# Second attention: row sums by a product with ones and one division for eight heads, in place of normalised exponentials

## What is computed

```python
qkv = hidden_states @ qkv_w + qkv_b          # [4, 256, 3 * 512]
q, k, v = split into 32 heads of D = 16
q, k = rope(q), rope(k)
scores = einsum('bqhd,bkhd->bhqk', q, k) / sqrt(16)
scores = scores + (1 - causal) * -66504.0
probs = softmax(scores, axis=-1)
ctx = einsum('bhqk,bkhd->bqhd', probs, v).reshape(b, s, 512)
return ctx @ out_w + out_b
```

## Time and profile before

| | |
|---|---|
| runs | 1877.82 us, the median of 3 (1872.31 to 1882.22) |
| profiled execution | 1872.54 us |
| its span, first to last instruction | 1870.7 us |
| busy in the span | TensorE 1760.0, VectorE 1115.4, ScalarE 1087.4, GpSimd 912.1 us |
| the second attention's steps | about 1555 to 1789 us |
| instructions | 32100 |

### The profile page before, as it was taken

One profiled execution on the slowest core, in us unless ns is written; L12 is line 12 of the kernel. 1 busy time (PEld: TensorE's weight loads), 2 busy tenths in 40 slices (PEclk: granted clock), 3 DMA queues, 4 the chain that ended last, 5 costly groups with the idle time before them and its releaser, 6 DMA issues.

```text
span 1870.7 us, 32100 instructions
## 1 busy us (share of the span) xinstructions
PE 1760.0 (94%) x11076; PEld 1527.0 (82%) x11076; DVE 1115.4 (60%) x3334; ACT 1087.4 (58%) x3071; POOL 912.1 (49%) x1153
## 2 busy tenths in 40 slices
PE   7979999999999999999999999999989788898788
PEld 6769989989998998998999899899878566666566
DVE  5655565556456556555644655654566777777656
ACT  3346565566556656556655765655632446777843
POOL 4545544555444555455554555545522336668720
PEclk9999999999999999999999999999989998999999
DMA  4300021012002001101200210110110310000001
GB/s 136 108 16 18 6 69 35 1 46 63 1 18 74 18 6 62 41 1 40 65 6 18 61 31 1 58 51 1 35 57 23 96 46 1 2 1 24 18 7 45
DMA packets 35424, 65.78 MB, mean 35 GB/s; under 512 B 4032, under 2 KB 4672, under 8 KB 35264
## 3 DMA queue, kind: packets, MB, share of 16 engines
q1 hardware_dynamic: 35264, 63.73, 10.8%
HBM read 61.62 MB, written 2.10 MB: 34 GB/s over the span
## 4 chain that ended last, share of the span: by engine, by line
PE 71%; DVE 9%; ACT 8%; issue 7%; POOL 5%; DMA 0%; SPq 0%; POOLq 0%; DVEq 0%; ACTq 0%
PE bank L357 55%; PE bank L974 5%; PE bank L961 4%; PE bank L976 3%; ACT s L1079 2%; POOL s L1795 2%; PE bank L1510 1%; PE bank L1481 1%; PE bank L1497 1%; DVE h L676 1%; ACT s L1566 1%; ACT W L256 1%; POOL WF L269 1%; POOL W L269 1%; POOL rstd L322 1%
## 5 line engine op out<-in xcount | busy, mean ns | idle before, releaser
L357 PE MATMUL bank<-W,oT 128*128 128x512 f32 x1632 | 432.7, 401 | 1.0 <-DVE oT L1747 1.0
L1286 POOL TENSOR_TENSOR qk<-work,qk 128x512 fp32r<-128x512 f32 (+1 forms) x160 | 193.5, 1209 | 445.9 <-ACT qk L1070 445.9
L357 PEld LDWEIGHTS bank<-W,oT 128*128 128x128 f32 x1632 | 290.1, 190 | 49.3 <-issue 1.3
L1086 ACT COPY pt<-bank 128x384 f32<-128x384 f32 x256 | 122.1, 477 | 329.8 <-PE bank L961 329.5
L1079 ACT ACTIVATE s<-s,neg_max 128x128 f32<-128x128 f32 (+1 forms) x512 | 227.6, 445 | 54.3 <-DVE neg_max L1193 52.1
L1278 POOL TENSOR_TENSOR work<-work,table 128x512 f32<-128x512 f32 (+1 forms) x160 | 191.3, 1196 | 139.1 <-ACT work L1065 139.1
L357 PE MATMUL bank<-W,xnA 128*128 128x320 f32 (+1 forms) x1056 | 186.3, 333 | 3.2 <-DVE xnA L342 2.9
L1170 DVE TENSOR_TENSOR work<-bank,table 128x512 f32<-128x512 f32 (+1 forms) x160 | 102.0, 637 | 132.3 <-ACT work L1065 132.3
L357 PEld LDWEIGHTS bank<-W,xnA 128*128 128x128 f32 x1056 | 166.8, 188 | 16.6 <-DVE xnA L342 4.1
L357 PE MATMUL bank<-xnA,W 128*128 128x256 f32 (+1 forms) x1080 | 162.1, 300 | 8.2 <-DVE W L262 6.8
L357 PE MATMUL bank<-xnB,W 128*128 128x256 f32 (+1 forms) x1080 | 164.3, 302 | 3.3 <-DVE xnB L342 3.3
(11 more groups left out here) (106 smaller groups left out, 3507.3 us busy)
## 6 DMA issues: line engine op xcount, KB each, us to landing
raw<-in_weights SPq DMA_DIRECT2D x215, 256.0 KB, 2.7
x<-in_x SPq DMA_DIRECT2D x8, 256.0 KB, 4.8
out<-x SPq DMA_DIRECT2D x8, 256.0 KB, 2.0
row<-in_bias_rows SPq DMA_DIRECT2D x5, 256.0 KB, 2.7
table<-in_constants SPq DMA_DIRECT2D x4, 240.0 KB, 3.2
b_qk<-in_bias_rows SPq DMA_DIRECT2D x1, 512.0 KB, 3.6
b_val<-in_bias_rows SPq DMA_DIRECT2D x1, 256.0 KB, 3.0
table<-in_constants SPq DMA_DIRECT2D x1, 66.0 KB, 2.3
```

Of the source, the lines that this page charges most:

```text
L357: last = nc.tensor.matmul(out_ap, lhs(i), rhs(j), start=start and k == 0, stop=stop and k == 2)
L1086: nc.scalar.copy(pt0[:, k, :], bank[PT][:, 0:3 * P]).then_inc(a_pt, 1)
L1286: nc.gpsimd.tensor_tensor(lo, work[:, 2 + s, st.columns(what)], hi.bitcast(F32), ALU.subtract).then_inc(a_rope_lo, 1)
```

## The change

The exponentials are no longer normalised before they are turned. TensorE turns them as soon as they are there (`b_exp`), and weighs the values with them as they are. Behind each step's weighting stand eight more products: the turned exponentials once more, with a stationary matrix of ones (32 columns; in the even step ones in its first half and zeros in the other, in the odd step the other way round), into columns 256 to 511 of OUT1. So each of the 128 rows of the group's output has its own row sum beside it, in the same bank. When the group is done, VectorE takes the reciprocal of the 128x256 sums, multiplies the output by it into a buffer `o1` in SBUF, and hands the bank on (`b_divided`). ScalarE makes the high part from `o1`, and GpSimd the low part. The accumulator outputs of the exponentials, the small reciprocals and the normalisation are gone. `divided(n)` is true for all steps, since DIVIDED is 0. GpSimd sets the ones once, by four memsets ahead of step 0.

```diff
--- before.py
+++ after.py
@@ -192,6 +192,8 @@
             b_row_sum = sb(a, "b_row_sum", [P, 8, 2])
             b_inv_sum = sb(a, "b_inv_sum", [P, 8, 4])
             b_val = sb(a, "b_val", [P, DIM])
+            ones = sb(a, "ones", [P, 2, 2 * D1])
+            o1 = sb(a, "o1", [P, 2, SEQ])
 
         bank = [ctx.enter_context(nc.psum_tensor(f"bank{i}", [P, CH], F32)) for i in range(8)]
         ident = table[:, T_ID:T_ID + P]
@@ -1342,6 +1344,9 @@
         b_o_lo = sem("b_o_lo")
         b_out = sem("b_out")
         b_row = sem("b_row")
+        b_ones = sem("b_ones")
+        b_inverse = sem("b_inverse")
+        b_divided = sem("b_divided")
         b_added = sem("b_added")
         LN1 = 32
         LAST_AT = [20, 20, 21, 22, 23, 24, 25, 26, 27, 28, 29]
@@ -1351,6 +1356,7 @@
         QUADS = BATCH * PER_BATCH
         STEPS1 = QUADS + 1
         SLOTS = 8
+        DIVIDED = 0
         ORING = 6
 
         PROJ = [(0, 0), (1, 0), (0, 1), (1, 1), (2, 0), (2, 1)]
@@ -1390,6 +1396,19 @@
             FILL_USES += [fill_of(n)] if fill_of(n) else []
             FILL_USES += [("norm", *norm_of(n))] if norm_of(n) else []
         FILL_USES += [("out", BATCH - 1, 0)]
+
+        def divided(n):
+
+            return n >= DIVIDED
+
+        def sum_read(eng, group):
+
+            if group < 0:
+                return
+            if divided(2 * group):
+                eng.wait_ge(b_divided, group - DIVIDED // 2 + 1)
+            else:
+                eng.wait_ge(b_o_lo, group + 1)
 
         def norm_no(b, tt):
             return LN1 + 2 + 2 * b + tt
@@ -1445,7 +1464,7 @@
 
             group = GR1 * b + g
             pe.wait_ge(b_rope, rope_no(b, 3) + 1)
-            at_least(pe, b_o_lo, group - 1)
+            sum_read(pe, group - 2)
             for j in range(2):
                 for tt in range(2):
                     c = j * DIM + g * P
@@ -1488,7 +1507,7 @@
                 group, odd = divmod(m, 2)
                 if not odd:
                     pe.wait_ge(b_v, group + 1)
-                    at_least(pe, b_o_lo, group)
+                    sum_read(pe, group - 1)
                     pe.wait_ge(b_q, min(group + 2, QUADS // 2))
                 for s in b_pt:
                     pe.wait_ge(s, 2 * (m + 1))
@@ -1497,14 +1516,22 @@
                         last = nc.tensor.matmul(bank[OUT1][rows(j), tt * P:SEQ],
                                                 vz[:, group % 2, odd, tt, 32 * j:32 * (j + 1)],
                                                 pt1[:, j, tt * 2 * P:(tt + 2) * P],
-                                                start=odd == 0 and tt == 0, stop=odd == 1 and tt == 1)
+                                                start=odd == 0 and tt == 0,
+                                                stop=odd == 1 and tt == 1 and not divided(m))
+                if divided(m):
+                    pe.wait_ge(b_ones, 4)
+                    for tt in range(2):
+                        for j in range(4):
+                            last = nc.tensor.matmul(bank[OUT1][rows(j), SEQ + tt * P:2 * SEQ], ones[:, odd, :],
+                                                    pt1[:, j, tt * 2 * P:(tt + 2) * P],
+                                                    start=False, stop=odd == 1 and tt == 1)
                 if odd:
                     last.then_inc(b_pv, 1)
 
             def turn(m, j):
                 if m == 0 and j < 2:
                     pe.wait_ge(b_biased, 5 + j)
-                pe.wait_ge(b_norm, 4 * m + j + 1)
+                pe.wait_ge(b_exp if divided(m) else b_norm, 4 * m + j + 1)
                 at_least(pe, b_pt[j % 2], 2 * m + j // 2)
                 for blk in range(3):
                     last = nc.tensor.transpose(bank[PTB[j % 2]][:, blk * P:(blk + 1) * P],
@@ -1563,9 +1590,12 @@
                 s = (4 * n + j) % SLOTS
                 act.wait_ge(b_min, 4 * n + j + 1)
                 for qt, cols in ((0, slice(0, P)), (1, slice(P, 3 * P))):
-                    last = nc.scalar.activation(s1[:, s, cols], s1[:, s, cols], ACT.Exp,
-                                                bias=b_neg_max[:, s, qt:qt + 1], scale=-1.0,
-                                                accum_out=b_row_sum[:, s, qt:qt + 1])
+                    bias = b_neg_max[:, s, qt:qt + 1]
+                    if divided(n):
+                        last = nc.scalar.activation(s1[:, s, cols], s1[:, s, cols], ACT.Exp, bias=bias, scale=-1.0)
+                    else:
+                        last = nc.scalar.activation(s1[:, s, cols], s1[:, s, cols], ACT.Exp, bias=bias, scale=-1.0,
+                                                    accum_out=b_row_sum[:, s, qt:qt + 1])
                 last.then_inc(b_exp, 1)
 
             here, before = n < QUADS, n >= 1
@@ -1583,8 +1613,12 @@
                 exponentials(3)
             if before and n % 2 == 0:
                 group = n // 2 - 1
-                act.wait_ge(b_pv, group + 1)
-                nc.scalar.copy(oT1[HI][:, group % ORING, :], bank[OUT1][:, 0:SEQ]).then_inc(b_o_hi, 1)
+                if divided(n - 1):
+                    act.wait_ge(b_divided, group - DIVIDED // 2 + 1)
+                    nc.scalar.copy(oT1[HI][:, group % ORING, :], o1[:, group % 2, :]).then_inc(b_o_hi, 1)
+                else:
+                    act.wait_ge(b_pv, group + 1)
+                    nc.scalar.copy(oT1[HI][:, group % ORING, :], bank[OUT1][:, 0:SEQ]).then_inc(b_o_hi, 1)
             if here:
                 b_pt_copy(act, n, 0)
                 b_pt_copy(act, n, 1)
@@ -1731,7 +1765,7 @@
                 b_vector_keys(dve, *prep_of(n - 1))
             if before:
                 b_pt_copy(dve, n - 1, 3)
-            if here:
+            if here and not divided(n):
                 inverses(0)
             if roped:
                 b_vector_cosine(dve, *roped)
@@ -1739,9 +1773,17 @@
                 b_vector_apply(dve, *norms_after(n - 1))
             if fill and fill[0] == "proj":
                 b_vector_biased(dve, *fill[1:])
-            if here:
+            if here and not divided(n):
                 inverses(1)
-            if before and n % 2 == 0:
+            if before and n % 2 == 0 and divided(n - 1):
+                group = n // 2 - 1
+                dve.wait_ge(b_pv, group + 1)
+                at_least(dve, b_o_lo, group - 1)
+                nc.vector.reciprocal(o1[:, group % 2, :], bank[OUT1][:, SEQ:2 * SEQ]).then_inc(b_inverse, 1)
+                dve.wait_ge(b_inverse, group - DIVIDED // 2 + 1)
+                nc.vector.tensor_tensor(o1[:, group % 2, :], bank[OUT1][:, 0:SEQ], o1[:, group % 2, :],
+                                        ALU.mult).then_inc(b_divided, 1)
+            elif before and n % 2 == 0:
                 group = n // 2 - 1
                 dve.wait_ge(b_o_hi, group + 1)
                 nc.vector.tensor_tensor(oT1[LO][:, group % ORING, :], bank[OUT1][:, 0:SEQ],
@@ -1765,6 +1807,10 @@
                 ln_power(pool, norm_no(0, i), i)
             pool.wait_ge(row_loaded, 16 * 4)
             pool.wait_ge(b_zero, 2)
+            for odd in range(2):
+                for half in range(2):
+                    nc.gpsimd.memset(ones[:, odd, half * D1:(half + 1) * D1],
+                                     1.0 if half == odd else 0.0).then_inc(b_ones, 1)
             for n in range(STEPS1):
                 b_gpsimd_step(pool, n)
 
@@ -1812,15 +1858,21 @@
                 b_sine(pool, *roped[1:])
             if n < QUADS and s in VALUES_AT:
                 values(VALUES_AT[s])
-            if n < QUADS:
+            if n < QUADS and not divided(n):
                 normalise(0)
                 normalise(1)
             if n < QUADS and s in (2, 4):
                 tt = s // 2 - 1
                 nc.gpsimd.tensor_tensor(tile_of(b, tt), tile_of(b, tt), row[:, :], ALU.add).then_inc(b_row, 1)
-            if n < QUADS:
+            if n < QUADS and not divided(n):
                 normalise(2)
                 normalise(3)
+            if n >= 1 and n % 2 == 0 and divided(n - 1):
+                group = n // 2 - 1
+                pool.wait_ge(b_o_hi, group + 1)
+                nc.gpsimd.tensor_tensor(oT1[LO][:, group % ORING, :], o1[:, group % 2, :],
+                                        oT1[HI][:, group % ORING, :].bitcast(F32),
+                                        ALU.subtract).then_inc(b_o_lo, 1)
             for i in norms_after(n)[1] if norms_after(n) else ():
                 ln_power(pool, norm_no(norms_after(n)[0], i), i % 2)
             for i in last_splits(n):
```

## The result

The changed kernel takes 1913.4 us, the median of four runs (1909.1 to 1913.9), against 1878.8 for the kernel before: a ratio of 1.0187 (95% interval 1.0163 to 1.0210), so 31 to 39 us slower. A second series gave 1.0207 (1.0185 to 1.0230). The forecast was 33 us slower, 1907 us, with a range of 1886 to 1924. The profiled execution took 1912.97 us.

A forecast was written before the change was run, and what follows sets the result against it. TensorE was taken as the bound. Terms 25.3 + 1.5 + 1.2 + 3.75 + 3.0 + 1.05 + 2.2 - 3.0 - 2.0 gave +33 us: 1905.5 on the profiled execution, 1910.8 on the median; predicted 1907, range 1886 to 1924.

The forecast's parts named there:

- Ones, 25.3 forecast: Eight more TensorE products ahead of the scores in each of 32 steps: +25.3 us, lower end 23.0.
- the row of the same form, 0.79: The weighting's 0.79 us from its start to the scores, taken as the cost of each step's products with ones.
- The reciprocal, 1.55 forecast: VectorE's reciprocal of 256 columns after every second step, from medians of short reciprocals: 1.55 us, bounds 0.80 to 2.4.
- estimate of 2.1 us: The large reciprocal at eight cycles of 0.96 GHz an element: 2.1 us, the sum 9 us higher.
- Even steps: Division alone in steps 2, 10, 12, 18, 20 and 28, followed by a projection: 0.25 us each, +1.5.
- steps 4, 24 and 26: No projection follows; copies, norm or minima are on the path of the division: 1.0 us each, +3.0.
- 14 and 22 by 1.9 and 6: Steps with moments behind the division on VectorE, then minima, exponentials, masks, weighting: 1.25 us each, +3.75.
- 8 and 16: Steps with norm, then projection; the norm's cast is late behind ScalarE's copies: 0.6 us each, +1.2.
- The gain, 5 forecast: Time won back: 3.0 us from GpSimd's normalisation, 2.0 from accumulator reads at 0.4 in steps 5, 6, 14, 22, 30.
- the transposing matmuls waited 7.2 us in all: TensorE's transposes waited 7.2 us for GpSimd's normalisation; about 3 us credited, in steps 21, 28 and 31.
- 10.5 for the steps: The division's delays in the even steps: 1.5, 1.2, 3.75 and 3.0 us, and 1.05 in step 30.
- The end, 3.0 forecast with its ones: Behind the last weighting: division, cast and GpSimd's subtraction take 3.3 us where 1.1 stood, +2.2 without the ones.
- rival 3: New waits of ScalarE in light steps drop TensorE's clock in eight more such steps: +12, 1918 us; chance 0.10.

The follow-up runs named there:

- the first run: The kernel before, still normalised, with the products with ones added behind each weighting and their result unused: ratio 1.0091, median 1890.8 us.

## Why the prediction was right

The direction and the mechanism were right: both new costs were put where they are, and TensorE's plain odd steps pay for the ones in full. The size was right in part by luck: the ones were put 4.5 us too dear and the division, less what it relieves, 6.5 too cheap, which mostly cancelled, and 3 us at the end were missing. The medians are 34.6 us apart. The two profiled executions are 40.4 us apart: 32.1 in the 31 steps, 6.1 behind them, and 3.0 ahead of the first weighting, which starts anywhere from 1565.7 to 1573.9 us in the traces of these kernels.

- **Ones, 25.3 forecast.** They cost 0.65 us and not 0.79, and 32 x 0.65 = 20.8. The steps bear that out, and the first run's +17 does within its interval. The prediction called itself wrong if the odd steps grew by clearly less than 0.7; they grew by 0.65 in all eight, within 0.01, so this term stands just under its own mark. The step that failed is the term "the row of the same form, 0.79", and its lower end of 0.72 as well: six transposes were no floor for eight products of the same columns. From weighting to ones it is 0.67, from ones to scores 0.76, from weighting to scores it was 0.79. So a group of products costs some 0.1 us less ahead of one in the same tiling mode. That agrees with the drain that the Trainium skill (TensorEngine Tiling (Array Packing), Key Properties) names for a change of mode; no run changes the mode alone, so the cause is not shown.
- **The reciprocal, 1.55 forecast, 1.76 measured,** inside 0.80 to 2.4. Two short reciprocals gave a good slope: 5.5 ns an element against (1757 - 166)/254 = 6.3. That is some six times the 1 ns of a copy, which fits an iterated operation. The prediction's estimate of 2.1 us, eight cycles for the repeat count of 8 in the Trainium skill (VectorE: DVE Perf Modes, First, the fixed hardware budget), is too high: the Trainium skill states the count there and no time, and the row decides.
- **Even steps.** Plain ones 8.35, forecast 8.2; steps 4, 24 and 26 grew by 1.84, 1.89 and 1.83, forecast 1.8; 14 and 22 by 1.9 and 6 by 1.2, forecast 1.6 (1.25 and 0.79, less 0.4); 8 and 16 by 1.6, forecast 1.4. The delays behind the division are of the forecast size in each. That ScalarE's queue is on the path is shown for the plain even steps and not for 4, 6, 14 and 22 (the run with the high part later).
- **The gain, 5 forecast, 12 measured.** The step that failed is "the transposing matmuls waited 7.2 us in all", of which it credited 3. The weight loads of the same line waited 19.9 us for GpSimd:

```profile
L1510 PEld LDWEIGHTS bank<-table,s 128*128 128x128 f32 x384 | 42.4, 146 | 33.3 <-POOL s L1795 19.9 <-issue 11.3
```

  In a plain even step 0.69 us came back, where the listed waits of the matmuls were 0.45. Steps 5, 21, 23, 25, 28 and 31 gave back 1.2 to 1.6 each, of which the prediction credited 21, 28 and 31.
- **Division and gain together.** Against the kernel without normalisation the changed one is 44.0 us longer over the 31 steps (251.6 - 207.6), of which the ones are 20.2 (31 x 0.65), so the division costs some 24 us, where the sum had 10.5 for the steps. (The copy in its place leaves 22.3 us, ones and some 2 more.) But the sum set the division against even steps that still held GpSimd's waits, and so had taken part of the gain into it. Net of the gain, division and relief came to 12 us in the steps (24 - 12) and were forecast at 5.5 (10.5 - 5); the ones, 4.5 too dear, covered most of the difference. Some 1.3 of the 12 are the clock in step 27 and not a wait: it grew by 1.91 us, the ones by 0.65 of that, at a granted clock of 0.84 where it was 1.00.
- **The end, 3.0 forecast with its ones, 6.1 measured** (14.53 from the last weighting to the next block, 8.45 before). The output products start 3.3 us later, where 3.0 was worked out. The other 2.8 are the output products at a granted clock of 0.65 (1.00 before). This is rival 3 in another place.

The numbers of the table and the runs add up so: 1862.0 without normalisation; 25.5 more with ones, a cheap division and its end (1887.5); 22 more for the reciprocal (1909.6).

## What to carry to other kernels

Work moved from an engine with slack to the one that sets the pace is paid in full there, while the engine relieved gives back only the waits it had caused: here 12 us came back for 163 us of GpSimd's and ScalarE's work, while the ones, 20.8 us of matmuls, cost 17 us where the old waits still stood and 0.65 each in the odd steps, which had none to give. Before taking an operation that acts on few columns to one that acts on many, measure its cost an element: a reciprocal of 256 columns was four times a copy. And where a bank and two queues wait for one instruction, find the length that other work hides: here two passes of 0.42 us were hidden in the plain even steps, and of the 1.33 that the reciprocal took beyond its pass 1.24 went on the path.

## What the runs showed of the hardware

- The reciprocal of 128x256 in float32 took 1757 ns (1756 to 1758), a copy of the same columns 425, so 6.3 ns an element beyond the fixed part (from 2 to 256 elements); a copy has about 1 (550 ns for 128x384, and (550 - 425)/128).
- Four exponentials with their four accumulator reads took 1.77 us in the chain before; without the reads, the start of the four and that of the copy behind them are 1.40 us apart (the rows below). So a read cost 0.09 us and not its 0.19, which makes the 0.4 us of the forecast 0.37.

```profile
1721.82 1.50 ACT L1595 ACTIVATE s<-s,b_neg_max 128x128 f32<-128x128 f32 x4
1723.22 0.47 ACT L1586 COPY pt<-bank 128x384 f32<-128x384 f32 x1
```

- Eight column-tiled products (128x32 stationary, 16 records) took 0.79 us up to the row-tiled scores behind them; eight more of the same form added 0.65.
- The 24 output products behind the last step took 5.72 or 5.73 us at a granted clock of 1.00 in three kernels. In all the others they took 7.28 to 8.53 us at 0.77 to 0.65, so TensorE was at its lower level for part of them. A wait of 1.03 us stands ahead of them in both sorts.
